# GNN edge loop: pairs gathered once, and the aggregation's one-hot rows taken from TensorE

## What is computed

```
h = layernorm(x) @ W.T                      # 6250 nodes, 8 heads of 32
alpha = a_src . h[src] + a_dst . h[dst] + relu(edge_attr @ edge_W.T + edge_b) . h[dst]
alpha = leaky_relu(alpha, 0.2)              # one number for each edge and head
attn = segment_softmax(alpha, dst)          # over the edges of one target
x = x + segment_sum(h[src] * attn, dst) + bias
x = x + moe(layernorm(x))                   # 8 experts, top 2, gelu
```

## Time and profile before

| | |
|---|---|
| median of the runs | 2148.92 us |
| the profiled execution, its own time | 2149.51 us |
| its span, first to last instruction | 2147.7 us |
| mean granted TensorE clock | 0.978 |
| edge loop, first to last gather issued | 83.9 to 1204.8 us |

### The profile page before, as it was taken

How to read it: one execution, slowest core, us unless ns; L and a number is a source line. 1 busy time by engine, 2 the same in 40 slices (tenths; PEclk the granted TensorE clock), 3 DMA queues, 4 the chain that set the end, 5 groups by cost and what they waited for, 6 DMA issues and landing times. The chain is left out here.

```text
span 2147.7 us, 38725 instructions
## 1 busy us (share of the span) xinstructions
PE 2012.5 (94%) x11620; PEld 1587.2 (74%) x11620; DVE 1539.7 (72%) x3628; ACT 1286.4 (60%) x3520; POOL 1284.1 (60%) x1224
## 2 busy tenths in 40 slices
PE   7799999999999999999999766899999999999997
PEld 6566666666666666666666534799999999999996
DVE  7389999999999999999999797644444444444442
ACT  4688788787787887887877655533323233332332
POOL 2377777777777777777777300255555555555553
PEclk9899999999999999999999977999999999999999
DMA  9766556556555565565555687422222222222221
GB/s 262 211 189 180 174 169 180 171 171 179 171 170 170 172 180 171 170 179 171 169 171 165 225 270 232 39 40 35 40 36 37 39 35 40 35 38 38 35 40 23
DMA packets 164108, 280.48 MB, mean 131 GB/s; under 512 B 36736, under 2 KB 115361, under 8 KB 163778
## 3 DMA queue, kind: packets, MB, share of 16 engines
q0 software_dynamic: 66720, 149.75, 29.6%
q1 hardware_dynamic: 88618, 121.01, 18.0%
q10 hardware_dynamic: 8568, 7.25, 1.0%
HBM read 240.94 MB, written 36.97 MB: 129 GB/s over the span
## 5 line engine op out<-in xcount | busy, mean ns | idle before, releaser
L667 POOL DMA_INDIRECT arena<-h_tab,src x880 | 854.0, 970 | 312.5 <-issue 243.8
L1646 ACT ACTIVATE arena<-psum,arena 128x128 f32<-128x128 f32 x840 | 239.5, 368 | 520.1 <-PE psum L1596 520.1
L833 PE MATMUL psum<-arena 128*128 128x256 f32 x1760 | 478.1, 395 | 1.4 <-issue 1.2
L854 PE MATMUL psum<-arena 128*128 128x264 f32 x1760 | 476.6, 395 | 0.7 <-DVE arena L945 0.7
L1596 PEld LDWEIGHTS psum<-arena 128*128 128x128 f32 x3360 | 394.2, 193 | 7.5 <-issue 2.2
L1596 PE MATMUL psum<-arena 128*128 128x128 f32 x3360 | 394.8, 276 | 1.8 <-DVE arena L1668 1.8
L854 PEld LDWEIGHTS psum<-arena 128*128 128x128 f32 x1760 | 322.0, 191 | 95.9 <-issue 45.4
L1612 PE MATMUL psum<-arena 128*128 x1680 | 379.8, 379 | 0.0
L833 PEld LDWEIGHTS psum<-arena 128*128 128x128 f32 x1760 | 317.4, 191 | 82.7 <-issue 39.6
L1558 POOL DMA_INDIRECT out_rows<-arena,src x105 | 212.9, 2027 | 247.5 <-DVE arena L1681 244.7
L1612 PEld LDWEIGHTS psum<-arena 128*128 128x128 f32 x1680 | 311.1, 190 | 38.0
(11 more groups left out here) (225 smaller groups left out, 1798.5 us busy)
## 6 DMA issues: line engine op xcount, KB each, us to landing
arena<-rel_list SPq DMA_DIRECT2D x110, 512.0 KB
arena<-in_W SPq DMA_DIRECT2D x16, 1024.0 KB, 12.4
arena<-h_tab,src POOLq DMA_INDIRECT x880
arena<-ea_slots SPq DMA_DIRECT2D x440, 27.0 KB
arena<-in_x SPq DMA_DIRECT2D x12, 896.0 KB, 8.9
h_tab<-arena SPq DMA_DIRECT2D x6, 924.0 KB, 8.7
out_rows<-arena SPq DMA_DIRECT2D x5, 896.0 KB, 5.3
xn<-arena ACTq DMA_DIRECT2D x5, 896.0 KB, 6.7
```

The source lines that it names most:

```text
L667: pool.indirect_dma_start(rows[:, s % RING, k, :], None, d.h_tab[:, :], bass.IndirectOffsetOnAxis(ap=c.src[:, s * U + k:s * U + k + 1], ax ...
L833: last = nc.tensor.matmul(ps[:, HDT + x, y * UE:(y + 1) * UE], hj[:, (s // 2 * 2 + y) % HJ, x * P:(x + 1) * P], oht[:, half % OT, (u + y) ...
L854: last = nc.tensor.matmul(ps[:, AGG + a % 2, 0:HS], oh[:, a % OH, k, :], rows[:, a % RING, k, :], start=(k == 0), stop=(k == U - 1))
L1646: last = nc.scalar.activation(hT[:, b, h * P:(h + 1) * P], ps[:, UP + 2 * b + half, h % 4 * P:(h % 4 + 1) * P], ACT.Gelu, bias=b1_now[:, b ...
```

## The change

Four things change in the edge loop, and `prepare` makes what they need.

- Pairs, not slots, are gathered: 784 gathers instead of 880, into a ring of 18 pairs. A slot finds its pair through registers loaded from lists (`spots`, `t_next`, `last`). Rows are 272 words instead of 264 (each head has a one, 32 values and the source's logit). A pair is told to be there (`rows_in`) by POOL itself, after it has issued the two pairs behind it. The place is free when DVE's `message` has read it.
- `message` writes to a buffer of its own (`msg`, two deep), with the ones taken along, and reads its factors from SBUF.
- ACT copies the sources' logits out of the ring slot by slot (`sources`), where DVE's `logits` read them from the ring.
- `one_hot` of two slots is one Relu of 128x512 out of PSUM. What it reads is made on PE by `mark`: four bf16 matmuls, with 5 rows, 128x128 each, which give 1 - (n - target)^2 from the target and the high and low bf16 part of its square. SP loads the three rows of target parts for each four slots (`marks`). `mark` and `to_rows` share the PSUM bank EX.

```diff
--- before.py
+++ after.py
...
+FW = D + 2
+TW = H * FW
+GK = 5
...
-RING, RENC, HJ, OH, OT, EB = 20, 5, 4, 4, 3, 3
+RING, RENC, HJ, OH, OT, EB, MSG = 18, 5, 4, 4, 3, 3, 2
...
-GATS = 6
+GATS = 3
+LAPS = PAIRS // RING
+MARK_WORDS = 4 * UE // 2
...
-                for rows, table in ((dst_rows, dst_pairs), (src_rows, src_pairs)):
-                    pool.indirect_dma_start(rows[:, g, :].bitcast(I32), None, table, bass.IndirectOffsetOnAxis(ap=t_col_i[:, g:g + 1].bitcast(I32), axis=0)
-                                            ).then_inc(lists_gathered, 16)
+                pool.indirect_dma_start(dst_rows[:, g, :].bitcast(I32), None, dst_pairs, bass.IndirectOffsetOnAxis(ap=t_col_i[:, g:g + 1].bitcast(I32), axis=0)
+                                        ).then_inc(lists_gathered, 16)
...
+            sp.wait_ge(t_made, 5)
             with nc.allow_non_contiguous_dma(reason="column to row"):
-                sp.dma_start(d.slot_j.rearrange("(g p) -> p g", p=P), j_col_i.bitcast(I32)).then_inc(t_stored, 16)
-            sp.wait_ge(t_stored, 16)
-            sp.dma_start(c.slot_j[:, :], d.slot_j.rearrange("(a s) -> a s", a=1)).then_inc(t_stored, 16)
+                for r, of_slots in enumerate((j_col_i, spot_i, t_next_i)):
+                    sp.dma_start(d.slots[r].rearrange("(g p) -> p g", p=P), of_slots.bitcast(I32)).then_inc(t_stored, 16)
+            sp.wait_ge(t_stored, 16 * 3)
+            sp.dma_start(c.slots[96:97, 0:PAIRS], last_i.bitcast(I32)).then_inc(t_stored, 16)
+            for r in range(3):
+                sp.dma_start(c.slots[32 * r:32 * r + 1, :], d.slots[r:r + 1, :]).then_inc(t_stored, 16)
...
+            sp.wait_ge(parts_made, 11)
+            for part, rows in enumerate((near, square_high, square_low)):
+                sp.dma_start(d.parts[part].rearrange("(g p e) -> p g e", p=P, e=UE), rows).then_inc(c.parts_stored, 16)
+            for r in range(4):
+                sp.dma_start(c.grid[32 * r:32 * r + GK, :], grid_row[0:1, :].rearrange("a (k n) -> a k n", k=GK)).then_inc(small_loaded, 16)
+            sp.wait_ge(t_stored, 16 * 7)
+            sp.wait_ge(small_loaded, 16 * 19)
...
+            def target_parts():
+
+                nc.vector.tensor_scalar(near, rel, -1.0, float(P), ALU.max, ALU.min).then_inc(parts_made, 1)
+                dve.wait_ge(parts_made, 8)
+                nc.vector.tensor_tensor(square, near, near, ALU.mult).then_inc(parts_made, 1)
+                dve.wait_ge(parts_made, 9)
+                nc.vector.tensor_copy(square_high, square).then_inc(parts_made, 1)
+                dve.wait_ge(parts_made, 10)
+                nc.vector.tensor_tensor(square_low, square, square_high, ALU.subtract).then_inc(parts_made, 1)
...
+        rows = take(RING * U * TW)
+        msg = take(MSG * U * HS).rearrange("p (b k n) -> p b k n", b=MSG, k=U)
+        alpha = take(P)
...
+        red_of = lambda ch: renc[:, (CS // 2 * ch + CS // 2 - 1) % RENC, 0, :]
+        SOURCES = ((-3, (0, 1)), (-2, (2, 3)), (-1, (4,)), (0, (5,)), (1, (6,)), (2, (7,)))
...
+            def landed(p):
+
+                pool.wait_ge(gathered[p % GATS], (p // GATS + 1) * U * 16)
+                pool.sem_inc(rows_in, 1)
...
-            for s in range(SLOTS):
-                half = s // 4
-                if s % 4 == 0 and half >= 2:
-                    pool.wait_ge(gathered[(half - 2) % GATS], ((half - 2) // GATS + 1) * 4 * U * 16)
-                if s >= RING:
-                    pool.wait_ge(agg_done, s - RING + 1)
+            for p in range(PAIRS):
+                q = p - RING
+                if q >= 0:
+                    if q % CS == 0:
+                        last = load_words(nc, c.slots[96:97, q:min(q + CS, PAIRS)], mybir.EngineType.Pool, 1, SLOTS)
+                    pool.wait_ge(msg_made, 1)
+                    pool.wait_ge(msg_made, last[q % CS])
                 for k in range(U):
-                    pool.indirect_dma_start(rows[:, s % RING, k, :], None, d.h_tab[:, :],
-                                            bass.IndirectOffsetOnAxis(ap=c.src[:, s * U + k:s * U + k + 1], axis=0)).then_inc(gathered[half % GATS], 16)
+                    pool.indirect_dma_start(rows[:, (p % RING * U + k) * TW:(p % RING * U + k + 1) * TW], None, d.h_tab[:, :],
+                                            bass.IndirectOffsetOnAxis(ap=c.src[:, p * U + k:p * U + k + 1], axis=0)).then_inc(gathered[p % GATS], 16)
+                if p >= 2:
+                    landed(p - 2)
+            for p in range(PAIRS - 2, PAIRS):
+                landed(p)
 
...
+            def marks(half):
+
+                if half >= 4:
+                    sp.wait_ge(marked, 2 * (half - 3))
+                if half >= 2:
+                    sp.wait_ge(marks_loaded[half % 2], 16 * (half // 2))
+                r = 32 * (half % 4)
+                sp.dma_start(c.marks[r:r + 3, :], d.parts[:, half * 4 * UE:(half + 1) * 4 * UE]).then_inc(marks_loaded[half % 2], 16)
...
+                if g >= 8 and g % 4 == 0:
+                    act.wait_ge(back_done, g // 4 - 1)
...
-            def one_hot(a):
-
-                if a >= OH:
-                    act.wait_ge(agg_done, a - OH + 1)
-                for k in range(U):
-                    nc.scalar.activation(oh[:, a % OH, k, :], c.iota_row[:, :], ACT.Square, bias=c.nrel[:, a * U + k:a * U + k + 1]).then_inc(square_made, 1)
-                act.wait_ge(square_made, U * (a + 1))
-                nc.scalar.activation(oh[:, a % OH, :, :], oh[:, a % OH, :, :], ACT.Relu, bias=c.ones[:, 0:1], scale=-1.0).then_inc(oh_made, 1)
+            def one_hot(g):
+
+                act.wait_ge(marked, g + 1)
+                if 2 * g >= OH:
+                    act.wait_ge(agg_done, 2 * g - OH + 2)
+                nc.scalar.activation(oh[:, 2 * g % OH:2 * g % OH + 2, :, :], ps[:, EX, :].rearrange("p (b k n) -> p b k n", b=2, k=U), ACT.Relu).then_inc(oh_made, 1)
...
-            def weights(ch):
+            def rows_of(ch):
 
                 act.wait_ge(flipped, ch + 1)
-                for n, (u0, u1) in enumerate(parts(ch)):
-                    last = nc.scalar.copy(ring(ch, u0, u1)[:, :, HD:HS], ps[:, EX, u0 * U * H:u1 * U * H].rearrange("p (t h) -> p t h", h=H))
-                last.then_inc(ex_made, 1)
-
-            js = load_words(nc, c.slot_j[0:1, 0:CS], mybir.EngineType.Activation)
+                if ch >= 2:
+                    act.wait_ge(msg_made, CS * (ch - 1))
+                nc.scalar.copy(factors_of[:, ch % 2, :], ps[:, EX, 0:P]).then_inc(ex_made, 1)
+
+            def sources(ch, u):
+
+                act.wait_ge(rows_in, 1)
+                act.wait_ge(rows_in, t_next[u])
+                row = rows[:, ds(spots[u], U * TW)].rearrange("p (k h f) -> p k h f", k=U, f=FW)
+                nc.scalar.copy(alpha[:, u * U * H:(u + 1) * U * H].rearrange("p (k h) -> p k h", h=H), row[:, :, :, FW - 1]).then_inc(sources_made, 1)
...
-                if 0 <= a + 2 < SLOTS:
-                    one_hot(a + 2)
+                for ch in due(t, -3):
+                    spots = load_words(nc, c.slots[32:33, ch * CS:(ch + 1) * CS], mybir.EngineType.Activation, 0, (RING - 1) * U * TW)
+                    t_next = load_words(nc, c.slots[64:65, ch * CS:(ch + 1) * CS], mybir.EngineType.Activation, 1, PAIRS)
+                if a % 2 == 0 and 0 <= a + 2 < SLOTS:
+                    one_hot((a + 2) // 2)
+                for after, us in SOURCES:
+                    for ch in due(t, after):
+                        if ch:
+                            act.wait_ge(turned, ch)
+                        for u in us:
+                            sources(ch, u)
...
+            def mark(g):
+                half, y = divmod(g, 2)
+                if y == 0:
+                    pe.wait_ge(marks_loaded[half % 2], 16 * (half // 2 + 1))
+                if g:
+                    pe.wait_ge(oh_made, g)
+                    pe.wait_ge(ex_made, (g + CS // 2 - 1) // (CS // 2))
+                r = 32 * (half % 4)
+                for k in range(2 * U):
+                    e = (2 * y * U + k) * P
+                    last = nc.tensor.matmul(ps[:, EX, k * P:(k + 1) * P], c.marks[r:r + GK, e:e + P], c.grid[r:r + GK, :], start=True, stop=True)
+                last.then_inc(marked, 1)
+
...
-                pe.wait_ge(oh_made, a + 1)
+                pe.wait_ge(oh_made, a // 2 + 1)
                 pe.wait_ge(msg_made, a + 1)
                 if a >= 2:
                     pe.wait_ge(acc_made, a - 1)
                 for k in range(U):
-                    last = nc.tensor.matmul(ps[:, AGG + a % 2, 0:HS], oh[:, a % OH, k, :], rows[:, a % RING, k, :], start=(k == 0), stop=(k == U - 1))
+                    last = nc.tensor.matmul(ps[:, AGG + a % 2, 0:HS], oh[:, a % OH, k, :], msg[:, a % MSG, k, :], start=(k == 0), stop=(k == U - 1))
...
-                if ch:
-                    pe.wait_ge(msg_made, CS * ch)
+                g = (CS * (ch + 2) - LAG + 2) // 2
+                if g >= 0:
```

(30 more changed lines are left out.)

212 lines of the change are left out of this document (110 added, 102 removed).

## The result

The changed kernel takes 2226.4 us (median of 4 runs, 2223.2 to 2228.4), the kernel before 2149.2 beside it: 1.0354 times as long, with an interval from 1.0342 to 1.0367. It is 77 us slower; the forecast was 2236. (In the jobs of e1 to e7 the kernel before itself took 2524 or 2545 us, so only their ratios are used, and those with care.)

The account below looks back on a forecast made before the run. PE was taken to bound the kernel, back to back but for a hole before to_rows. 2149.5 + 116 (marks) - 36 (wait that goes) + 6 (before the loop) = 2235.5, say 2236 us; range 2195 to 2290 us.

Parts of the forecast that it names:

- The bound: Edge loop: PE works back to back, 20.3 us a chunk, with about 0.6 us of wait before to_rows.
- Marks, +116: Edge loop on PE: 220 mark blocks of 0.53 us, 0.31 for entering and leaving and 0.22 content, +116 us.
- Dearer marks: Rival, marks on PE: weight loads not hidden, block 0.74 us, +46, 2282 us; chance 13%.
- cheap marks: Rival, marks on PE: entering and leaving costs nothing, 2168 us; chance 6%.
- The wait that goes, -36: PE's hole before to_rows (L884) in the loop: 33.0 us of wait and a few more go, -36 us.
- The gathers: POOL in the loop: 96 of 880 gathers go, 121 us of its time, giving only the hole at L884.
- Some 19.4 with gaps: DVE in the loop: its pace a chunk in us, next if gathers set the pace and PE had room.
- ACT: One-hot rows in the loop: ACT saves about 5.6 us a chunk, counted as zero for the time.
- Before the loop, +6: End of prepare: new stores and copies behind the last table store delay the barrier, 0 to 10 us, taken as +6.
- After the loop, 0: Stages after the loop: sums are read with another stride, no change counted.
- Gathers as the pace and room for marks: Rival, edge loop: gathers set the pace and marks fit in PE's idle time, 2100 us; chance 6%.
- In-order waits: Rival, edge loop: new waits on in-order queues, 55 us if short by 1 us a chunk, 2290 us; chance 14%.

Follow-up runs that it names:

- e1: Changed kernel with all mark blocks but the first left out, the same kernel as e9: ratio 0.9914 in a job where the kernel before took 2524 us.
- e7: Changed kernel with mark moved directly behind encode, the same kernel as e10: ratio 1.0017 in a job where the kernel before took 2524 us.
- e10: Changed kernel with mark moved directly behind encode, same rows of the array, nothing left out: 2167.7 us, ratio 1.0072.
- e11: Changed kernel with mark directly behind encode, on array rows this encode doesn't use, and the new small DMAs issued earlier in prepare: 2154.4 us, ratio 1.001.
- e12: Kernel before with 15 gathers in a chunk instead of 16, nothing else changed: 2128.3 us, ratio 0.9894.
- e9: Changed kernel with 219 of the 220 mark blocks left out, their signals and waits kept: 2149.5 us, ratio 0.9987.
- e8: Changed kernel with its stores of target parts and four copies to grid issued earlier in prepare: 2221.8 us, ratio 1.0326.

## Why the prediction was right, point by point

The main term, the marks on a full PE, was right in kind and size. That the sum came within 10 us is in part luck: the wait that goes was put 13.5 us too small, and what lies before and behind the loop 7.2 us too small, and these cancel by half. What ended the wait was also read wrongly.

**The bound.** Right. PE was the fullest engine and became the only one that matters: 21.6 us in every chunk, no wait.

**Marks, +116.** Right, +115.3 (220 x 0.524). By its parts: the share of entering and leaving was put at 0.31 and the content at 0.22. Measured are 0.098 before the block, 0.104 in the `expand` group behind it, and 0.322 between, of which four starts of 56 ns are 0.22; the rest, 0.10, is the late start of `expand`. That makes 0.30 and 0.22. (The sign that was named for it, 0.5 to 0.6 us from the first start of the marks to `expand`, was not met: it is 0.32, and the 0.5 holds only with the parts before and behind.) e10 and e11 show that these are two costs and not one: the first is paid once for `encode` and `mark` together, the second goes as well where the rows differ. The figure of 81 ns a matmul in the Trainium skill, TensorE: Matmul & The Clock Gate, section Back-to-back issue gap, isn't met in this stream: 56 ns. The other statement, in the Trainium skill, TensorEngine Tiling (Array Packing), section Key Properties, that a change of mode drains the engine, agrees with the 0.30 us. Dearer marks (2282) and cheap marks (2168) are both refuted by this.

**The wait that goes, -36.** The step that was too small: 1161.2 - 1097.5 = 63.7, less 216 x 0.524 = 113.2 for the marks in between, is -49.5 us. The prediction took the 33.0 us of idle time in the groups and some 4 for the part of a pass under which a wait is hidden. In the changed kernel that part can be measured, since nothing waits there: `to_rows` starts 0.22 us after the last pass of `aggregate`, while that pass is listed as 0.39 us. Before, the distance was 0.66 to 1.59. So a wait hides 0.17 us a chunk, not 0.07, and the waits before `to_rows` sum to 40.8 us. Most of the remaining 9 lies in the last chunk, which takes 21.3 us before and 16.7 in the changed kernel with its marks. PE's own work was 19.5 us a chunk, not 19.7.

The reading of the cause was wrong too. The prediction lets L884 wait for ACT's exponentials and looks for the hole in the chain gathers, logits, scans, exponentials. The wait ended with `message` in every chunk but the first, 0.35 us after the exponentials alone would have let `to_rows` go. The late gathers made only what lies above 0.44 us a chunk (e12). The change removes the wait for `message` and the gathers together, so the forecast that the hole goes was right by more than the reason it gave.

The forecast was too high by 9.1 us (2235.5 against 2226.4). The terms give 7.0: 13.5 here and 0.7 at the marks (116 against 115.3), less 3.8 before and 3.4 after the loop. The other 2 are the profiled execution's distance from the median (2228.4 against 2226.4).

**The gathers.** The direction is right: POOL set the last part of the pace, and POOL waits for DVE now. That it alone stood between 20.3 and 19.7 is wrong: e12 shows 20.0 with the gathers out of the way, and e9 20.1, both with DVE busy 843 to 847 of 900 us and a hole at PE.

**DVE.** "Some 19.4 with gaps" was too low; the paces with a way through DVE are 20.0 and 20.1. It cost the forecast nothing, as 21.6 is above both, but it made the expectations of e9's 2111 us and of e11 wrong. They are two paces rather than one: in e12 PE waits before `to_rows` for `message`, in e9, which has no such wait, before `expand` for `product`. `message` takes 702 ns against the 696 worked out: right. No experiment shortened DVE's own work, so that DVE, with its way over ACT and PE, sets the 20.0 is read from waits and busy time, not shown by taking it away.

**ACT.** Counted as zero, right: its busy time in a chunk fell from 16.3 us to 11.4 (627.3 / 55), and nothing of the end follows it. `one_hot` takes 600 ns (587 expected).

**Before the loop, +6.** Right in kind, +10.3 in size, of which 0.5 is the first mark block. The upper bound of 10 was the better guess: all seven DMAs are issued after the last table store, and the barrier and the first loads stand behind them. e8 gives 4.6 of it back.

**After the loop, 0.** +5.0 from the last `to_rows` on. 2.3 of it lie in the last steps of the loop, up to the last `aggregate` (12.2 us after the last `to_rows` instead of 9.9), where three mark blocks make 1.6; the remaining 2.7 were not looked into.

**The rivals.** Gathers as the pace and room for marks: refuted by PE at 899.89 of 900. In-order waits: refuted by the flat chunks without idle time at PE, and by e9. A rival that the prediction didn't have stands untested: that a part of the hole goes by the new factors in SBUF and not by the fewer gathers. e12 tests the gathers alone.
